# Row tails divided on GpSimd, one slot order for all engines, one filler matmul per site

## The reference, cut to what matters

```python
# layer 0: normalise and modulate, then sparse attention (8 heads)
scores = (q_c . k_c + q_r . key_r) * scale      # the index picks 96 keys for each query
attn   = softmax(scores); x += gate * (attn @ v) @ W_out
# then a modulated block of two sub-layers, each:
sim  = q @ k^T * 8, local window of 64 keys back; attn = softmax(sim)   # 8 heads of 64
x    = x + (attn @ v) @ wo
x    = x + (a * gelu(g)) @ w2                   # a, g = layernorm(shift(x)) @ w1
# layer 1: 16-head attention over all 256 tokens, then 16 experts (8 chosen) + 1 shared
x += gate * (softmax(q k^T / sqrt(8)) @ v) @ W_out
x += gate * (shared(x) + sum_e route_e * expert_e(x))
```

## Time and profile before

| | |
|---|---|
| median of 3 runs | 1540.81 us (1538.6 to 1547.84) |
| the profiled execution, time | 1539.22 us |
| its span, first to last instruction | 1537.4 us |
| busy: PE, DVE, ACT, POOL | 1346.2, 903.6, 862.0, 361.0 us |
| of PE's: the fillers of line 550 | 297.9 us, 2038 matmuls |
| mean granted clock of TensorE | 0.978 of full speed |

### The profile page before, as it was taken

The page is one execution under the profiler, slowest core; times in us unless marked ns, Lnnn a source line. Parts: engine busy times, 40 slices in busy tenths (PEclk is TensorE's granted clock), DMA queues, the critical chain, the costliest instruction groups (busy, mean ns, idle before and its releaser), DMA issues. The chain is left out here.

```text
span 1537.4 us, 30694 instructions
## 1 busy us (share of the span) xinstructions
PE 1346.2 (88%) x11816; PEld 963.9 (63%) x11816; DVE 903.6 (59%) x2934; ACT 862.0 (56%) x2231; POOL 361.0 (23%) x580
## 2 busy tenths in 40 slices
PE   6789989898898998888898899988899899888797
PEld 5456657566665666665676566666676566556576
DVE  3855575745565756565366566556456655666634
ACT  3444666554544657555565375754665536665483
POOL 0422040211332222210153124030024320402002
PEclk9999999999999999999999999999999899999999
DMA  8121000000112100000011200000001210000000
GB/s 274 51 64 28 7 1 1 1 4 1 49 29 58 21 5 1 1 1 5 8 46 29 61 17 1 1 1 1 4 8 44 73 28 9 1 1 1 1 1 8
DMA packets 45618, 36.46 MB, mean 24 GB/s; under 512 B 32992, under 2 KB 37536, under 8 KB 44960
## 3 DMA queue, kind: packets, MB, share of 16 engines
q1 hardware_dynamic: 45472, 34.50, 7.9%
HBM read 25.46 MB, written 7.44 MB: 21 GB/s over the span
## 5 line engine op out<-in xcount | busy, mean ns | idle before, releaser
L1114 ACT ACTIVATE arena<-ps 128x512 f32<-128x512 f32 (+7 forms) x560 | 252.7, 482 | 229.9 <-PE ps L688 33.9
L550 PE MATMUL ps<-mean_mat 128*128 128x256 bf16 x2038 | 297.9, 279 | 5.7 <-DVE arena L1484 3.2
L550 PEld LDWEIGHTS ps<-mean_mat 128*128 128x128 bf16 x2038 | 189.7, 99 | 94.4 <-issue 56.5
L1892 POOL TENSOR_TENSOR arena<-arena 128x512 f32<-128x512 f32 x64 | 81.3, 1272 | 460.9 <-DVE arena L1497 460.4
L1320 ACT ACTIVATE arena<-arena,small 128x192 f32<-128x192 f32 (+1 forms) x256 | 129.8, 510 | 34.4 <-DVE small L1669 34.0
L1717 DVE TENSOR_REDUCE small<-ps 128x4 f32<-128x1024 f32 x64 | 75.3, 1219 | 24.2 <-PE ps L986 23.9
L1607 DVE TENSOR_TENSOR gath<-ps,rank_tab 96x512 f32<-96x512 f32 x96 | 63.3, 684 | 42.9 <-PE ps L578 42.6
L1770 DVE TENSOR_TENSOR arena<-arena,ps 128x512 f32<-128x512 f32 x64 | 42.9, 687 | 73.1 <-ACT arena L1414 57.9
L1477 DVE CUSTOM_DVE_ANT_0 arena<-ps,mask_w_bf 128x192 f32<-128x192 f32 (+1 forms) x256 | 67.4, 319 | 21.4 <-PE ps L664 21.3
L1268 ACT ACTIVATE arena<-arena,small 128x224 f32<-128x224 f32 (+1 forms) x128 | 56.6, 444 | 40.7 <-DVE small L1626 40.6
L757 PE MATMUL ps<-w_experts,arena 128*128 128x128 f32 x544 | 69.8, 280 | 10.3 <-DVE arena L1770 6.8
(11 more groups left out here) (279 smaller groups left out, 2915.5 us busy)
## 6 DMA issues: line engine op xcount, KB each, us to landing
idxb<-idx_scratch SPq DMA_DIRECT2D x24, 512.0 KB, 5.1
score_scratch<-arena SPq DMA_DIRECT2D x96, 64.0 KB, 1.7
w_experts<-in_experts SPq DMA_DIRECT2D x3, 1088.0 KB, 16.5
w_wqkv<-in_wqkv SPq DMA_DIRECT2D x1, 1536.0 KB, 9.7
arena<-score_scratch SPq DMA_DIRECT2D x96, 16.0 KB, 2.1
arena<-arena SPq DMA_DIRECT2D x96, 16.0 KB, 1.8
arena<-in_x SPq DMA_DIRECT2D x8, 128.0 KB, 2.2
out_x<-arena SPq DMA_DIRECT2D x8, 128.0 KB, 1.9
```

Of the source, the lines that this page charges most:

```text
L550: mm(to, still[:, 0:P], still, start=True, stop=True)
L1114: return act.activation(dst, src, ACT.Copy)
L1892: ins = pool.tensor_tensor(own, own, turned, ALU.add)
```

## The change

The diff has three parts. `slot_order` no longer takes an engine: all five engines follow one order, which is made from a list of slots with a duration each (266.5 us for one sequence) by always taking the stream whose clock is behind; stream 1's clock starts at 45 us, and only the stream whose turn it is may enter F9. Both strings of `BUSY` become ones, so every site issues one filler. And the tail product moves from VectorE to GpSimd (`normed_tail`): VectorE signals the reciprocals of u = 2 and 3 with `u_recip` and waits for that signal itself, GpSimd waits for it too, multiplies, and signals `u_tail`; PE waits for `u_tail` between the four transposes and the two of the tail.

```diff
--- before.py
+++ after.py
@@ -94,52 +94,48 @@
     return c
 
 
-LAYER = ["Q0", "Q1", "Q2", "Q3", "Q4", "W0", "W1", "W2", "W3", "W4", "W5", "M0"]
-SLOTS = (["F0", "N0a", "N0b"] + [f"F{i}" for i in range(1, 11)] + [f"G{i}" for i in range(8)] + [f"A{i}" for i in range(9)]
-         + ["N1a", "N1b"] + [name + ".0" for name in LAYER] + ["N2a", "N2b", "M1.0", "M2.0"]
-         + [name + ".1" for name in LAYER] + ["N3a", "N3b", "M1.1", "M2.1"]
-         + ["N4a", "N4b"] + [f"X{i}" for i in range(14)] + ["N5a", "N5b"] + [f"E{i}" for i in range(7)])
-TURNS = {
...
-}
-
-
-def slot_order(engine):
-
-    order, done, s = [], [0] * NS, 0
-    for turn in TURNS[engine]:
-        for _ in range(int(turn, 36)):
-            order.append((s, SLOTS[done[s] % len(SLOTS)]))
-            done[s] += 1
-        s = (s + 1) % NS
+LAYER = [("Q0", 3.5), ("Q1", 4.0), ("Q2", 3.5), ("Q3", 4.0), ("Q4", 2.5),
+         ("W0", 2.5), ("W1", 3.3), ("W2", 3.3), ("W3", 3.5), ("W4", 3.0), ("W5", 2.0), ("M0", 2.2)]
+SLOTS = ([("F0", 1.2), ("N0a", 1.2), ("N0b", 2.0), ("F1", 3.5), ("F2", 2.2), ("F3", 2.5), ("F4", 2.8), ("F5", 2.8),
+          ("F6", 2.8), ("F7", 2.8), ("F8", 4.0), ("F9", 5.0), ("F10", 4.0),
+          ("G0", 2.5), ("G1", 2.6), ("G2", 2.6), ("G3", 3.0), ("G4", 2.6), ("G5", 3.5), ("G6", 3.5), ("G7", 3.0),
+          ("A0", 3.0), ("A1", 4.0), ("A2", 4.0), ("A3", 4.0), ("A4", 4.0), ("A5", 2.5), ("A6", 4.0), ("A7", 2.5), ("A8", 2.5),
+          ("N1a", 1.2), ("N1b", 2.5)]
+         + [(name + ".0", us) for name, us in LAYER] + [("N2a", 1.2), ("N2b", 2.0), ("M1.0", 3.0), ("M2.0", 2.5)]
+         + [(name + ".1", us) for name, us in LAYER] + [("N3a", 1.2), ("N3b", 2.0), ("M1.1", 3.0), ("M2.1", 2.5)]
+         + [("N4a", 1.2), ("N4b", 2.0), ("X0", 3.0), ("X1", 3.0), ("X2", 3.0), ("X3", 3.0), ("X4", 3.0), ("X5", 2.5),
+            ("X6", 3.0), ("X7", 3.0), ("X8", 2.5), ("X9", 3.0), ("X10", 3.0), ("X11", 2.5), ("X12", 3.0), ("X13", 1.8),
+            ("N5a", 1.2), ("N5b", 2.0), ("E0", 4.0), ("E1", 5.5), ("E2", 6.5), ("E3", 6.5), ("E4", 6.5), ("E5", 3.5),
+            ("E6", 2.0)])
+LAG = 45.0
+
+
+def slot_order():
+
+    where = [0.0, LAG]
+    left = [[(name, us) for r in range(ROUNDS) for name, us in SLOTS] for s in range(NS)]
+    gathered = 0
+    order = []
+    while any(left):
+        ready = [s for s in range(NS) if left[s]]
+        can = []
+        for s in ready:
+            name = left[s][0][0]
+            turn = gathered % NS == s
+            if name == "F9" and not turn:
+                continue
+            can.append(s)
+        s = min(can, key=lambda i: where[i])
+        name, us = left[s].pop(0)
+        if name == "G7":
+            gathered += 1
+            where[1 - s] = where[1 - s] if left[1 - s] and left[1 - s][0][0] != "F9" else max(where[1 - s], where[s])
+        where[s] += us
+        order.append((s, name))
     return order
 
 
-BUSY = [("b0935960007c4ac4135003003811ba0000000201570058454437c00100418390040003500277001305071c906060500620431495211001"
...
+BUSY = ["1" * 400] * NS
 
 GATHERED = ["gscore_mm", "gathT_mm"]
 EXPERT_MM = ["e_gate", "e_gate", "e_up", "e_up"]
@@ -174,7 +170,7 @@
 }
 GROUP = {name: group for group, names in IN_ORDER.items() for name in names}
 ALONE = {"x_loaded": 16, "kv_split": 5, "q_ready": 2, "idx_saved": 32, "idx_part0": 16, "idx_part1": 16, "idx_part2": 16, "gsc_saved": 192, "gsc_back0": 64,
...
+         "gsc_back1": 128, "xg_loaded": 192, "ln_out": 6, "u_mm": 12, "u_bias": 12, "u_exp": 12, "u_recip": 6, "u_tail": 6, "u_prob": 12,
          "u_turned": 18, "u_pt_act": 12, "u_pt_dve": 6, "u_pv": 12, "u_out": 12, "x_own": 2, "e_pool": 4, "y_ready": 1,
          "y_stored": 16}
 
@@ -461,7 +457,7 @@
             for r in range(ROUNDS):
                 b = NS * r + s
                 of.r = r
-                for name in SLOTS:
+                for name, _ in SLOTS:
                     if name == "F8":
                         sp.wait_ge(*at("top_ready", 1))
                         first = LW * RANKS
@@ -530,7 +526,7 @@
             for dst, src in late_loads:
                 sp.dma_start(dst, src).then_inc(sig("late_loaded"), 16)
             streams = [sync_stream(sp, s) for s in range(NS)]
-            for s, name in slot_order("sp"):
+            for s, name in slot_order():
                 assert next(streams[s]) == name
             for s in range(NS):
                 sp.wait_ge(sig(f"y_stored{s}"), 16 * ROUNDS)
@@ -625,6 +621,7 @@
                 last.then_inc(*one("u_turned"))
                 if T == 1:
                     pe.wait_ge(*at("u_out", 4 * g + u))
+                    pe.wait_ge(*at("u_tail", 2 * g + u - 1))
                     for i in range(2):
                         last = pe.transpose(bank[3][:, 256 + P * i:256 + P * i + P], tail[:, cols(i)], ident[:, :])
                     last.then_inc(*one("u_turned"))
@@ -1088,7 +1085,7 @@
             pe.wait_ge(sig("packed_loaded"), 16 * PACKED_LOADS)
             pe.wait_ge(sig("centered"), 1)
             streams = [tensor_stream(pe, s) for s in range(NS)]
-            order = slot_order("pe")
+            order = slot_order()
             for i, (s, name) in enumerate(order):
                 if i == order.index((0, "N0b")):
                     absorb()
@@ -1430,7 +1427,7 @@
             act.preload_act_table_set(LN_AND_EXP)
             act.wait_ge(sig("cols_set"), 4)
             streams = [scalar_stream(act, st, s) for s in range(NS)]
-            order = slot_order("act")
+            order = slot_order()
             for i, (s, name) in enumerate(order):
                 if i == order.index((0, "F1")):
                     act.wait_ge(sig("absorbed"), 1)
@@ -1459,14 +1456,15 @@
 
             def normed(g, u, probs, tail):
                 dve.wait_ge(*at("u_exp", 4 * g + u + 1))
-                st.link(dve.reciprocal(rl[s][:, u, :], ls[s][:, u, :]))
+                ins = dve.reciprocal(rl[s][:, u, :], ls[s][:, u, :])
+                if u < 2:
+                    st.link(ins)
+                else:
+                    ins.then_inc(*one("u_recip"))
+                    dve.wait_ge(*at("u_recip", 2 * g + u - 1))
                 first = 0 if g == 0 or u < 2 else WMAX - P
                 part = probs[:, :, first:first + P]
                 ins = dve.tensor_tensor(part, part, bc(rl[s][:, u, :], 2, P), ALU.mult)
-                if u >= 2:
-                    rest = probs[:, :, P:WMAX] if g == 0 else probs[:, :, 0:first]
-                    ins = dve.tensor_tensor(tail.rearrange("p (h n) -> p h n", h=4), rest,
-                                            bc(rl[s][:, u, :], 2, WMAX - P), ALU.mult)
                 if g == 0:
                     part = probs[:, :, keys(u // 2):]
                     ins = dve.tensor_tensor(part, part, bc(rl[s][:, u, :], 2, RANKS), ALU.mult)
@@ -1852,7 +1850,7 @@
                 dve.wait_ge(sig("tables_set"), 2)
 
             streams = [vector_stream(dve, st, s) for s in range(NS)]
-            order = slot_order("dve")
+            order = slot_order()
             for i, (s, name) in enumerate(order):
                 if i == order.index((0, "F1")):
                     absorbed()
@@ -1905,6 +1903,12 @@
                 own = m.own[k][:, 512:].rearrange("p (h n) -> p h n", h=H)
                 pool.tensor_tensor(own, own, bc(g[:, H:], 2, DH), ALU.mult).then_inc(*one("k_ready"))
                 pool.tensor_scalar(cqs[s][:, k, :], g[:, 0:H], 8.0, None, ALU.mult).then_inc(*one("rs_final"))
+
+            def normed_tail(g, u, probs, tail):
+                pool.wait_ge(*at("u_recip", 2 * g + u - 1))
+                rest = probs[:, :, P:WMAX] if g == 0 else probs[:, :, 0:WMAX - P]
+                pool.tensor_tensor(tail.rearrange("p (h n) -> p h n", h=4), rest,
+                                   bc(rl[s][:, u, :], 2, WMAX - P), ALU.mult).then_inc(*one("u_tail"))
 
             for r in range(ROUNDS):
                 of.r = r
@@ -1931,6 +1935,8 @@
                 for i in range(8):
                     yield f"G{i}"
                 for i in range(6):
+                    if i in (3, 4):
+                        normed_tail(0, i - 1, m.probs_a[1][:, 4 * (i - 3):4 * (i - 3) + 4, :], m.tail_a[i - 3])
                     if i == 5:
                         pool.wait_ge(*at("gsc_saved", 192))
                         pool.memset(m.pdiag, 0.0).then_inc(*one("pdiag_zero"))
@@ -1949,6 +1955,10 @@
                     yield f"Q3.{l}"
                     yield f"Q4.{l}"
                     for i in range(6):
+                        if i in (3, 4):
+                            n = keys(1)
+                            probs = m.probs_w[(i - 1) % 3][:, 0:4 * n].rearrange("p (h n) -> p h n", h=4)
+                            normed_tail(1 + l, i - 1, probs, m.tail_w[(i - 1) % 2])
                         yield f"W{i}.{l}"
                     for name in ("M0", f"N{2 + l}a", f"N{2 + l}b", "M1", "M2"):
                         yield name + (f".{l}" if name[0] == "M" else "")
```

(15 more changed lines are left out.)

## The result

The changed kernel takes 1732.76 us (median, 1731.72 to 1738.18) against 1540.45: the ratio is 1.1249, 95% interval 1.1211 to 1.1288. It is slower by 192 us. I forecast slower, 1630, and a range up to 1725. The sign was right; the forecast had 89 us of the 192, less than half, and the time lies outside the range.

The account below looks back on a forecast made before the run. Bound by how soon each stream's next step finds its engine free, not by any one engine. Profiled 1539.2 + 0 - 20 + 38 + 18 + 57 - 4 (table loads) = 1628 us, 1630 as a median; range 1560 to 1725.

Parts of the forecast that it names:

- Part 1, tails: Tail products moved from VectorE to GpSimd: stretching gives back the 0.42 us won; 0, bounds -20 and +20 us.
- Part 2 and 3, fillers and clock: PE's 576 filler sites: 1462 fewer fillers save 20 us, and more cold-clock time on PE costs 38 us.
- my own sign: Mean granted clock of the changed kernel: if it falls under 0.88, the clock is the bound.
- Part 4 (b), a common order: All engines in one order: one in ten of some 591 places becomes a 0.96 us wait; +57, bounds 0 and +150.
- Part 4 (a): Both ends of the span: stream 1's larger lag adds 8 slots alone at each end, 2.3 us each; +18 us.
- The one that ends not slower: Whole kernel: fillers were in the way, clock holds, slack takes the common order; 1489 us; 0.13 together with a milder form.
- The clock rival: PE stretches rich in fillers go cold half of their time without them; 1744 us; chance 0.15.
- its clock term: In the clock rival, PE's filler-rich stretches at half clock half of their time: 154 us, in place of 38.
- The collision of the tails with `u_tail`: Tail products collide and GpSimd's queue adds a 1.27 us wait for each of 48 units; 1709 us; chance 0.07.

Follow-up runs that it names:

- The three settings: Tail products on GpSimd against VectorE: GpSimd alone following PE's string (1564.62 us); PE's string for all engines, old fillers (1587.91); the changed kernel against tails undone (1720.21).
- `after_fill4`: The changed kernel with four fillers at each site, 2304 in all: 1753.48 us, 1.1387 of the kernel before.
- `fillers_only`: The kernel before with one filler at each of its 576 sites, nothing else changed: 1554.47 us, 1.0088.
- `order_only`: The kernel before with the one common order made from the new list, old filler counts kept: 1738.06 us, 1.1300.
- `after_experts_short`: The changed kernel with the first five expert slots listed at 3.0 and 3.2 us in place of 4.0, 5.5 and 6.5: 1730.25 us, 1.1246.
- `after_x_long`: The changed kernel with the slots in which PE waits for VectorE's maxima listed 3.0 us longer each: 1740.73 us, 1.1293.

## Why the prediction was right in its sign and wrong in its size

**Part 1, tails, taken as 0.** The three settings average -3, but that is luck: they measured -4, -18 and +13, and no term of mine held the order they are in. The mechanism was half right. GpSimd's product is stretched, 1117 ns as a rule against 612 where VectorE does nothing, but VectorE's product that starts 0.05 us before it (line 1467, before 1465) stays at 0.69 us; I expected 1.1. I had read only half of my rows: in the earlier trace rows line 1465 started 0.06 us ahead of GpSimd and kept its 0.69 us, and the product stretched in the earlier trace rows had started behind GpSimd's. In the sparse attention a third product (line 1470) follows while GpSimd is still at work, and that one is stretched, from 0.28 to 0.70 us, in 12 of the 16 units with a tail:

```profile
606.08 0.69 DVE L1467 TENSOR_TENSOR arena<-arena,small 128x512 f32<-128x512 f32 x1
606.12 1.11 POOL L1910 TENSOR_TENSOR arena<-arena,small 128x256 f32<-128x256 f32 x1 [14.76 <-DVE small L1459]
606.68 0.70 DVE L1470 TENSOR_TENSOR arena<-arena,small 128x128 f32<-128x128 f32 x1
```

So `u_prob` can come some 0.4 us sooner in the 32 units of the windows, and in those 12 it comes 0.07 us later (1.30 us behind the start of the first product, against 1.23 in the kernel before).

**Part 2 and 3, fillers and clock, +18 together.** Measured +14 in the old orders, +11 with PE's old order for all engines, and -18 with the list, each the net of both parts. The clock fell further than I put it for the forecast, to 0.877. That is below the 0.88 under which, by my own sign, the clock would be the bound, and it was not: four fillers a site brought it to 0.924 and lost 20 us. The busy time removed, 214 us, was off; it is 122. My 0.146 us was the mean over all fillers; one alone is 0.305, and a further one in a row adds 0.12 ((375.6 - 175.8) / 1728, from `after_fill4`).

**Part 4 (b), a common order, 57 us.** The size, 66 measured, was right in part by luck. I counted the places in which the old strings of PE, DVE and ACT differ, 0.94 and 0.72 slots on average. GpSimd's string, which I left out for its 460 us of waiting, lies 4.3 slots off PE's and costs 26 us alone. SyncE's lies 6.5 slots off and was never moved alone, so how the other 40 us divide among DVE, ACT and SP is not shown.

**Part 4 (a), the step that failed.** I priced the difference between the list and the old strings by the lag alone, 8 slots at 2.3 us, 18 us. The runs put it at 134, and it shows as 63 us in the first round, 52 in the three next, 21 at the end. (Of the 8 slots "at each end" there are 10 at the start, 7 to 17, and 6 at the end, 6 to 12; the sum is the same.) What stood in no term is what happens between the ends when a list places stream 1 elsewhere against stream 0. Shifts of the one stream show that this has the size: one slot costs 118 us, and lags of 20 and 80 add 69 and 38 us to the middle rounds. In the list's own durations stream 0's lead swung between 18 and 62 us in the old strings and is nearly constant in the new order; my term looked only at the slots alone at the two ends.

**The rivals.** The one that ends not slower fell with `fillers_only` and `order_only`. The clock rival gave 1744, near the measured time, for the wrong reason: without its clock term it stands at 1590, while `order_only` takes 1738 with all the fillers in place, and its clock fell to 0.926 all the same. One filler a site costs 14 us in the old orders. The collision of the tails with `u_tail` was seen, 28.8 us of wait, and moved to another wait when removed.

**What stays open.** Why just one slot costs 118 us: it is spread over many waits of PE, none of them above 16.5 us more, and what sets off each was not followed. That the list's durations can be fitted to lose little is shown; which of them matter is not. Two coarse guesses at it (`after_experts_short`, `after_x_long`) failed.

## What to carry to other kernels

Where two streams share in-order engines and one stream's work laid end to end fills the span, the order is a resource like an engine: price a change of order by shifting the old one by a step and measuring, not by counting slots alone at its ends. A long wait or a long stage in such a schedule can be where lost time shows and not where it is made, as twice here: check by removing it. Test a lightly used engine's order before giving it up: GpSimd's was worth 26 us at 23% busy.

## What the runs showed of the hardware

GpSimd's product of 128x256 from SBUF took 612 ns alone (4 times) and 1117 ns when a VectorE product with two SBUF operands had started 0.05 us ahead (44 times), and that VectorE product kept its 0.69 us. A VectorE product of 128x128 that started while GpSimd's ran took 0.70 us in place of 0.28 (12 times). In these rows and in the earlier trace rows the product that started first kept its time and the second paid. The columns are minimum, median and maximum ns:

```profile
L1910 POOL TENSOR_TENSOR arena<-arena,small x48: 612/1117/1120, 125.2 to 1597.1; 128x256 f32<-128x256 f32 x48
L1470 DVE TENSOR_TENSOR arena<-arena,small x32: 283/493/805, 104.6 to 1446.4; 128x128 f32<-128x128 f32 x32
```

With 1462 fillers fewer the granted clock went from 0.978 to 0.923 and the time rose by 0.9% in one order; with 1728 more it went from 0.877 to 0.924 and the time rose by 1.2% in another. The mean clock alone told the time in neither.
